# Two layers of state-space model, attention and expert layers on one core: products parted by tile, a second bank for results, constant products ahead of four stages

## The chip, the core and the metric

The kernel runs on one core of one Trainium2 chip, as one launch. The metric is the device time of an execution in microseconds; lower is better. TensorE (PE) multiplies; its weight loads are shown apart (PEld). VectorE (DVE), ScalarE (ACT) and GpSimd (POOL) do the elementwise work, and SyncE (SP) and POOL start transfers.

## The reference

4,096 tokens (8 batches of 512) of width 256 go through two layers. Each layer normalises `xn = layernorm(x)` and adds two branches to `x`:

```python
x = x + mamba(xn)     + one_expert_of_8(xn)             # layer 0
x = x + attention(xn) + two_of_8_experts(xn, capacity)  # layer 1
```

The part that the change touches most is the first branch, for each batch:

```python
z, xBC, dt = xn @ in_proj_w.T
xBC = silu(causal_conv4(xBC)); x, B, C (two directions) = xBC
Y   = ssd(x * dt, A * dt, B, C, chunk=128)        # chunks of 128 tokens, states between them
y   = shift(Y + x * D) forward + backward + x * repeat(x @ fc_D_w.T + D)
out = rmsnorm(y * silu(z)) * norm_w @ out_proj_w.T
```

The attention has 16 heads of width 16: scores of q and k, clipped, multiplied by a decay, clipped, softmax, times v, projected out.

## The kernel before, in words

The kernel is a row of stages, each a block in which every engine has its own instruction stream; a barrier stands between stages. In order: constants, `normalise` and `route` of layer 0 and the time steps (to 93 us of the profiled execution), `mamba` (to 760), `one_expert_each` (to 1084), `normalise` and `route` of layer 1 (to 1173), `project` (to 1276), `attend_and_experts` (to the end). Engines meet only through counting semaphores: `wait_ge` before an instruction, `then_inc` behind it. The order on each engine is the order in which the program is written; there is no planner.

**mamba.** A loop over the 8 batches; a tile is 128 tokens, so a batch has 4 tiles. On PE the function `turn(i, ahead)` makes one batch: the products for `z` (L920, 4 tiles), the turning of B (L931) and of the x rows (L940, one group of four transposes for each tile, copied out by ACT at L1138), the skip factors' products (L947, 8 columns wide, for all tiles into one small part of the bank `psG`), then `products` (C times B, L970), `grow` (the states, L963, three steps in two directions), `diagonal` (L981, then L986 for 8 heads, then L995) for u = 0 to 7 (tile u // 2, direction u % 2), `turn_tile` (L1007) and `output` (L1015) for each tile, and, between these at the end, `conv` (L907), the eight products that the next batch's convolution begins with. ACT makes the decay matrices (`decays`, L1113, 8 exponentials for each u, the first four u without a break). POOL multiplies the x rows by factors: `xdd` (L1204) for the states, `xdt` (L1211) and `xfd` (L1217) for the results. DVE sums neighbours (`near`, L1272), adds D to the skip factors (`fd`, L1275), masks and multiplies the decays (L1299, L1302), carries the states on (L1287 to L1292), and in `finish` reads the finished bank `psY` (L1327), adds and gates; `outputs` (L1342) adds the result to x. `other_taps` (L1255) is DVE's part of the convolution: six additions for each pair of channels' tiles, 128x512.

PSUM has eight banks, all in use: `psA` (two, turned rows and outputs), `psS` (two), `psG`, `psY`, `psO` (two). The convolution's products go round four banks, `psC` = `psS` (two), `psY`, `psA[0]`. Since there is one `psY`, PE's `diagonal` of a tile's first direction waits until DVE has read the tile before:

```python
pe.wait_ge(y_read, i * CPB + t)
```

**one_expert_each.** 39 tiles of rows sorted by expert. POOL issues 12 row fetches and the loads of the second weights before it marks the first expert's weights as there (L1461), and PE's first `down` (L1502) waits for that mark.

**project** makes q, k and v in parts and stores them. **attend_and_experts** goes through 512 tiles of scores in one skewed pipeline: `score` on PE runs 12 tiles ahead, `clip` (L2271) and `fade` (L2279) on DVE follow, `exp` (L2220) on ACT, `turn` (L2111) on PE, its copy (L2229) on ACT, `mix` (L2125); from tile 4 on, one job of the experts (L2163, L2170, L2177) stands behind every fourth tile. There are three score banks, so `score(3)` waits for the first clip. The block `v` (4,096 values a partition) is cleared by POOL's memset (L2072) behind the first loads that POOL issues, and DVE waits for `v_cleared` ahead of its first clip.

## Time and profile before

| | |
|---|---|
| median of 3 runs | 2097.98 us (2097.97 to 2099.04) |
| profiled execution, its own time | 2115.85 us |
| its span, first to last instruction | 2114.1 us |
| mean granted TensorE clock | 0.931 |
| PE busy | 1805.7 us (85%) |
| PEld busy | 1230.2 us (58%) |
| DVE busy | 1376.7 us (65%) |
| ACT busy | 1158.1 us (55%) |
| POOL busy | 419.7 us (20%) |

### The profile page before, as it was taken

The numbers are of one execution on the slowest core, as the hardware profiler recorded it, in microseconds if no ns is written. First come the engines' busy times: TensorE is split into PE (matmuls) and PEld (weight loads), VectorE is DVE, ScalarE is ACT, GpSimd is POOL, SyncE is SP. The second block draws the span as 40 slices with busy tenths as digits, with TensorE's granted clock in tenths as the row PEclk, the third lists the DMA queues.
The fourth block names the chain that finished last, engine by engine and source line by source line (L and its number), as shares of the span: only waits on it lengthen the run. The fifth ranks groups of instructions, "written<-read, shape, count | busy, mean of one in ns | idle before, by whom it ended". The sixth has DMA issues, their size and how long they took to land. (4 is left out here: it accounts for less than half of the span.)

```text
span 2114.1 us, 33649 instructions
## 1 busy us (share of the span) xinstructions
PE 1805.7 (85%) x9950; PEld 1230.2 (58%) x9950; DVE 1376.7 (65%) x3090; ACT 1158.1 (55%) x2806; POOL 419.7 (20%) x406
## 2 busy tenths in 40 slices
PE   5288898898899869899945695998989999999998
PEld 2246666656656669799932353564646565655555
DVE  5647667667667622122246686797878888888885
ACT  2154654664564612122212354888788888788886
POOL 2003313313413432422111202010010202020101
PEclk9589999999999989899977797999999999999999
DMA  4411211211211168455354294233333334333311
GB/s 168 147 59 62 89 63 66 94 65 59 100 68 50 60 223 281 161 175 175 131 160 160 75 296 130 70 82 72 98 72 85 98 84 104 80 91 81 81 31 31
DMA packets 143789, 226.10 MB, mean 107 GB/s; under 512 B 17725, under 2 KB 110015, under 8 KB 143648
## 3 DMA queue, kind: packets, MB, share of 16 engines
q1 hardware_dynamic: 124464, 179.95, 27.4%
q0 software_dynamic: 19184, 44.45, 8.2%
q8 instruction: 67, 1.10, 0.2%
q14 instruction: 74, 0.61, 0.1%
HBM read 174.26 MB, written 50.99 MB: 107 GB/s over the span
## 5 line engine op out<-in xcount | busy, mean ns | idle before, releaser
L2271 DVE TENSOR_SCALAR att_scores<-att_psS 128x512 f32<-128x512 f32 x512 | 349.6, 683 | 106.3 <-PE att_psS L2103 90.9
L2220 ACT ACTIVATE att_prob<-att_scores,att_shift 128x512 f32<-128x512 f32 x512 | 383.2, 748 | 30.7 <-DVE att_shift L2287 30.6
L2229 ACT COPY att_pT<-att_psT 128x512 f32<-128x512 f32 x512 | 305.9, 598 | 136.1 <-PE att_psT L2111 134.9
L2279 DVE CUSTOM_DVE_ANT_0 att_scores<-att_scores,first_decay 128x512 f32<-128x512 f32 x512 | 348.4, 681 | 0.0
L2111 PEld LDWEIGHTS att_psT<-ident,att_prob 128*128 128x128 f32 x2048 | 244.8, 142 | 159.4 <-issue 100.2
L2111 PE MATMUL att_psT<-ident,att_prob 128*128 128x128 f32 x2048 | 315.2, 277 | 15.4 <-ACT att_pT L2229 13.9
L2103 PE MATMUL att_psS<-first_ks,first_qs 128*128 128x512 bf16 x512 | 197.7, 387 | 27.8 <-DVE att_scores L2271 22.6
L1113 ACT ACTIVATE mamba_L<-mamba_am,mamba_minus 128x128 f32<-128x128 f32 x512 | 153.9, 388 | 59.3 <-PE mamba_psY L986 59.2
L2125 PE MATMUL att_psO<-att_pT,att_v 128*32 128x512 f32 x1024 | 139.7, 619 | 37.7 <-ACT att_pT L2229 37.7
L1488 PE MATMUL ffn_psH<-ffn_xT,ffn_w 128*128 128x128 f32 x1248 | 151.0, 280 | 5.0 <-issue 4.4
L1488 PEld LDWEIGHTS ffn_psH<-ffn_xT,ffn_w 128*128 128x128 f32 x1248 | 150.1, 196 | 8.6 <-issue 6.7
L1531 ACT ACTIVATE ffn_hT<-ffn_psH,ffn_b 128x128 f32<-128x128 f32 x156 | 44.6, 368 | 200.7 <-PE ffn_psH L1488 136.3
L1502 PE MATMUL ffn_psY<-ffn_w,ffn_hT 128*128 x624 | 146.0, 386 | 6.0 <-issue 4.9
L1552 DVE TENSOR_SCALAR ffn_hT<-ffn_psH,ffn_b 128x128 f32<-128x128 f32 x156 | 44.1, 345 | 164.0 <-PE ffn_psH L1488 124.6
L1502 PEld LDWEIGHTS ffn_psY<-ffn_w,ffn_hT 128*128 128x128 f32 x624 | 117.1, 193 | 23.4 <-issue 9.3
L986 PE MATMUL mamba_psY<-mamba_xdt,mamba_L 128*128 128x64 f32 x1024 | 121.2, 273 | 0.2 <-POOL mamba_xdt L1211 0.2
L986 PEld LDWEIGHTS mamba_psY<-mamba_xdt,mamba_L 128*128 128x128 f32 x1024 | 120.3, 193 | 0.8 <-issue 0.3
L2170 PE MATMUL att_psF<-att_xT,att_w 128*128 128x512 f32 x224 | 114.1, 634 | 0.0
L1204 POOL TENSOR_TENSOR mamba_xdd<-mamba_xl,mamba_dtdec 128x512 f32<-128x512 f32 x48 | 56.8, 1198 | 273.1 <-ACT mamba_xl L1138 235.2
L2220 ACT ACTIVATION_READ_ACCUMULATOR att_prob<-att_scores,att_shift 128x1 f32 x512 | 110.6, 216 | 0.0
L2177 PE MATMUL att_psF<-att_w,att_hT 128*128 128x256 f32 x448 | 108.5, 385 | 0.0
L2177 PEld LDWEIGHTS att_psF<-att_w,att_hT 128*128 128x128 f32 x448 | 84.5, 192 | 22.4 <-issue 12.2
(283 smaller groups left out, 2820.8 us busy)
## 6 DMA issues: line engine op xcount, KB each, us to landing
ffn_w<-in_w SPq DMA_DIRECT2D x39, 1024.0 KB
mamba_am<-a_rows SPq DMA_DIRECT2D x64, 512.0 KB, 3.8
first_qs<-q_parts SPq DMA_DIRECT2D x256, 64.0 KB
first_ks<-k_parts SPq DMA_DIRECT2D x256, 64.0 KB
xn<-xn_all SPq DMA_DIRECT2D x16, 512.0 KB, 5.8
ffn_w<-in_w POOLq DMA_DIRECT2D x8, 1024.0 KB, 6.1
att_w<-in_inter POOLq DMA_DIRECT2D x7, 1024.0 KB, 5.6
att_w<-in_outer POOLq DMA_DIRECT2D x7, 1024.0 KB
```

Source lines behind the costliest of these rows:

```text
L986: mm = nc.tensor.matmul(psY[:, h * HD:(h + 1) * HD], L[:, u % NL, h], xdt[:, u % 2, h * HD:(h + 1) * HD], start=False, stop=(d == 1), skip ...
L1113: ex = nc.scalar.activation(L[:, u % NL, h], am[:, u % NA, h * P:(h + 1) * P], ACT.Exp, bias=minus[:, d, t, h:h + 1])
L1488: mm = nc.tensor.matmul(psH[j % 2][hf][:, q], w1[:, j % NW, k, (hf * HALF + q) * P:(hf * HALF + q + 1) * P], xT[:, j % 2, k], start=(k == ...
L1502: mm = nc.tensor.matmul(psY[j % 2][:], hT[:, j % 2, f], w2[:, bass.ds(at * W2N + f * D, D)], start=(f == 0), stop=(f == FT - 1))
L2103: nc.tensor.matmul(psS[n % NS][:], qs[:, of % NQK, j, t * P:(t + 1) * P], ks[:, of % NQK, j, :], start=True, stop=True).then_inc(scored, 1)
L2111: mm = nc.tensor.transpose(ps[:, k * P:(k + 1) * P], prob[:, n % NP, k * P:(k + 1) * P], C.ident[:])
L2125: mm = nc.tensor.matmul(psO[STRIP * j:STRIP * (j + 1), :], v[:, b % 2, k, octet * QUAD + j, i], pT[:, (of * QUAD + j) % HEADS_T, k], start ...
L2177: mm = nc.tensor.matmul(psF[:, 0:D], hT[:, f, t * P:(t + 1) * P], w2[:, f], start=(f == 0), stop=(f == FT - 1), skip_group_check=True)
L2220: nc.scalar.activation(prob[:, n % NP], scores[:, n % NCL], ACT.Exp, bias=shift[:, h % 2, t:t + 1], accum_out=total[:, octet % 2, t, j, i: ...
L2229: nc.scalar.copy(pT[:, h % HEADS_T, :, t * P:(t + 1) * P], bank_of("turn", n)[:].rearrange("p (k q) -> p k q", k=CPB)).then_inc(pT_ready, 1)
L2271: vec.tensor_scalar(scores[:, n % NCL], psS[n % NS][:], -CLAMP, CLAMP, ALU.max, ALU.min).then_inc(clipped, 1)
L2279: vec.tensor_tensor_reduce(scores[:, n % NCL], scores[:, n % NCL], decay[:, FAR - t * P:FAR - t * P + SEQ], 1.0, -2.0 * CLAMP, ALU.mult, A ...
```

## The change

Five edits:

1. **Skip factors by tile.** `skips(t)` makes the eight instructions of one tile. Two tiles' stand between the turnings of the x rows, two behind the first two steps of `grow`. The rows are turned in the order 0, 3, 1, 2 (`TURN`); POOL begins each of its first four `xdd` when that tile's rows are there, not when all are. DVE's `fd` stands behind `grow(1)`.
2. **Two result banks.** `psG` is given up; its table moves to `psO[1]`, its skip factors to `psY[1]`. A tile's results go to `psY[t % 2]`.
3. **The convolution's fourth bank** is `psY[1]`, no longer `psA[0]`, so waits around `psA` change; the last `turn_tile` no longer waits for four results of the next batch's convolution.
4. **Constant products.** `keep_running` multiplies a block of ones by the identity into a bank whose content isn't needed: 16 times at the beginning of `mamba` and `one_expert_each`, 14 times in `project`, and 14 times in attention behind the third score. Nothing reads them.
5. **Attention's values cleared first.** POOL's memset stands ahead of its loads, and DVE waits for it in `spread_values(0)` (tile 6), no longer ahead of the first clip.

```diff
+def keep_running(nc, C, bank, times):
+    for _ in range(times):
+        nc.tensor.matmul(bank, C.ones[:], C.ident[:], start=True, stop=True)
...
+    TURN = [0, 3, 1, 2]
...
-        psG = s.psum("psG", [P, 512])
-        psY = s.psum("psY", [P, DI])
+        psY = [s.psum(f"psY{j}", [P, DI]) for j in range(2)]
...
-        psC = [ps[:].rearrange("p a b -> p (a b)") for ps in psS] + [psY[:], psA[0][:]]
+        psC = [ps[:].rearrange("p a b -> p (a b)") for ps in psS] + [ps[:] for ps in psY]
-        fd_ps = psG[:, 448:480].rearrange("p (c h) -> p c h", c=CPB)
+        fd_ps = psY[1][:, 0:CPB * NH].rearrange("p (c h) -> p c h", c=CPB)
-        psP = psG[:, 0:L0_TILES]
+        psP = psO[1][:, 0:L0_TILES]
...
+                keep_running(nc, C, psO[0][:, 0:P], 16)
...
-                    elif n == 2:
-                        pe.wait_ge(y_read, i * CPB)
-                    elif n == 3:
+                    elif n < 4:
                         if not_first:
-                            pe.wait_ge(yT_ready, i * CPB - 1)
+                            pe.wait_ge(y_read, i * CPB + n - 3)
...
-                    for t in range(CPB):
-                        use = XT_AT + t
+                    def turn_rows(k):
+                        use, t = XT_AT + k, TURN[k]
...
+                    pe.wait_ge(fd_ready, i)
+                    turn_rows(0)
+                    turn_rows(1)
+                    skips(0)
+                    turn_rows(2)
+                    skips(1)
+                    turn_rows(3)
...
-                            pe.wait_ge(y_read, i * CPB + t)
+                            if t >= 2:
+                                pe.wait_ge(y_read, i * CPB + t - 1)
+                            elif t == 1:
+                                pe.wait_ge(fd_ready, i + 1)
...
                     products(0)
                     grow(0)
+                    skips(2)
                     products(1)
                     grow(1)
+                    skips(3)
                     grow(2)
...
-                    turn_tile(CPB - 1, ahead)
+                    turn_tile(CPB - 1)
...
-                    pool.wait_ge(tok_ready, (i + 1) * (2 + CPB))
                     for k in range(CPB - 1):
                         for d in range(2):
                             n = 2 * k + d
+                            if n < CPB:
+                                pool.wait_ge(tok_ready, i * (2 + CPB) + 2 + n + 1)
...
-                    dve.wait_ge(fd_done, i + 1)
-                    dve.wait_ge(xfd_ready, i * CPB)
-                    v.tensor_tensor(fd[:], fd_ps, ...).then_inc(fd_ready, 1)
                     grow(1)
+                    dve.wait_ge(fd_done, (i + 1) * CPB)
+                    dve.wait_ge(xfd_ready, i * CPB)
+                    v.tensor_tensor(fd[:], fd_ps, ...).then_inc(fd_ready, 1)
                     grow(2)
...
+                keep_running(nc, C, psY[0][:, 0:P], 16)        # one_expert_each
...
+                keep_running(nc, C, psV[0][:, 0, 0:P], 14)     # project
...
+                nc.gpsimd.memset(v[:], 0.0).then_inc(v_cleared, 1)
                 load_rows(0)
                 load_w1(0)
                 load_w2(0)
-                nc.gpsimd.memset(v[:], 0.0).then_inc(v_cleared, 1)
...
+                        if n + SCORE == NS - 1:
+                            keep_running(nc, C, psF[:, 0:P], 14)
...
+                    if b == 0:
+                        dve.wait_ge(v_cleared, 1)
...
-                dve.wait_ge(v_cleared, 1)
```

## Rows read from the trace of the kernel before

**Rows 1.** The page: TensorE's granted clock in forty slices, in tenths
```profile
PEclk9589999999999989899977797999999999999999
```

**Rows 2.** PE's waits, 143 to 755 us: total us, times, longest
```profile
PE mamba_psY L981 <- DVE mamba_y L1327: 26.2, 24, 1.4
...
PE mamba_psO L963 <- POOL mamba_xdd L1204: 14.0, 8, 2.3
...
PE mamba_psA L1007 <- DVE mamba_acc L1255: 9.9, 7, 1.4
```

**Rows 3.** Timeline, PE, one batch: start, length, line, count, [idle before <-releaser]
```profile
384.25 3.80 PE L947 MATMUL mamba_psG<-mamba_w_fcd,mamba_xc 128*128 128x8 f32 x32
...
388.90 2.92 PE L963 MATMUL mamba_psO<-mamba_xdd,mamba_Bl 128*128 128x512 f32 x4
...
407.32 1.16 PE L981 MATMUL mamba_psY<-mamba_d_diag,mamba_near 128*128 128x128 f32 x8 [1.38 <-DVE mamba_y L1327]
...
433.14 3.60 PE L907 MATMUL mamba_psS<-mamba_xT,mamba_w_in 128*128 128x512 f32 x8
...
446.75 0.66 PE L1007 MATMUL mamba_psA<-ident,mamba_y 128*128 128x128 f32 x4 [1.41 <-DVE mamba_acc L1255]
```

**Rows 4.** Timeline, DVE, the same batch
```profile
389.70 1.23 DVE L1302 SCALAR_TENSOR_TENSOR mamba_L<-mamba_L,mamba_masked 128x1024 f32<-128x1024 f32 x1
...
408.63 1.22 DVE L1302 SCALAR_TENSOR_TENSOR mamba_L<-mamba_L,mamba_masked 128x1024 f32<-128x1024 f32 x1
```

**Rows 5.** Timeline, ACT, the same batch
```profile
385.06 1.28 ACT L1113 ACT_TABLE_LOAD   x1
...
386.35 9.46 ACT L1113 ACTIVATE mamba_L<-mamba_am,mamba_minus 128x128 f32<-128x128 f32 x32
```

**Rows 6.** Stretches: us; busy (count) of PE, PEld, DVE, ACT, POOL; granted clock
```profile
388.00:391.00 3.00, 3.00 (x8) 1.91 (x8) 1.92 (x4) 3.00 (x11) 0.10 (x1) 0.50 0.38 116
...
397.00:401.00 4.00, 3.65 (x10) 2.11 (x9) 3.67 (x6) 0.00 (x0) 3.73 (x3) 0.60 0.31 124
...
1288.00:1297.00 9.00, 4.84 (x8) 0.83 (x8) 9.00 (x23) 2.31 (x7) 0.00 (x0) 0.50 0.24 85
```

**Rows 7.** Timeline, beginning of the state-space stage
```profile
99.53 7.05 PE L387 MATMUL mamba_psG<-mamba_table_valued,mamba_table_hot_row 128*128 128x39 f32 x32 [7.39 <-POOL mamba_table_valued L366]
...
106.38 6.02 PE L907 MATMUL mamba_psS<-mamba_xT,mamba_w_in 128*128 128x512 f32 x8
...
113.24 4.28 DVE L1255 SCALAR_TENSOR_TENSOR mamba_acc<-mamba_psS,mamba_taps,mamba_acc 128x511 f32<-128x511 f32 x6 [10.01 <-ACT mamba_acc L1081]
...
115.66 1.87 PE L387 MATMUL mamba_psG<-mamba_table_valued,mamba_table_hot_row 128*128 128x39 f32 x16
```

**Rows 8.** Timeline, beginning of the one-expert stage
```profile
780.21 0.15 POOL L1461 MEMSET ffn_marked<- 128x1 f32 x1
...
780.50 3.72 PE L1502 MATMUL ffn_psY<-ffn_w,ffn_hT 128*128 x16 [1.05 <-POOL ffn_marked L1461]
```

**Rows 9.** ACT's waits, 755 to 1075 us: total us, times, longest
```profile
ACT ffn_hT L1531 <- PE ffn_psH L1488: 136.3, 29, 5.0
...
ACT ffn_hT L1531 <- DMA xnT<-norm_xT: 20.3, 1, 20.3
```

**Rows 10.** Timeline, PE, beginning of the projections
```profile
1178.44 1.97 PE L1729 MATMUL proj_psV<-proj_wd,proj_wkT 128*128 128x64 f32 x8 [16.03 <-DVE proj_wkT L1823]
...
1180.79 3.68 PE L1700 MATMUL proj_psL<-xT_all,proj_wkv 128*64 128x512 f32 x4 [0.38 <-DVE proj_wkv L1825]
...
1184.40 4.63 PE L1707 MATMUL proj_psQ<-xT_all,proj_wq 128*128 128x512 f32 x8
```

**Rows 11.** Timeline, beginning of attention
```profile
1276.61 1.44 PE L2103 MATMUL att_psS<-first_ks,first_qs 128*128 128x512 bf16 x3 [4.26 <-PEq L66]
...
1284.22 3.53 POOL L2072 MEMSET att_v<- 128x4096 f32 x1
...
1287.85 1.89 DVE L2271 TENSOR_SCALAR att_scores<-att_psS 128x512 f32<-128x512 f32 x3 [14.87 <-POOL att_v L2072]
```

More of the change, by code:

```diff
@@ L820, in drained @@
             if last < BT_AT:
-                eng.wait_ge(conv_done, (i + 1) * CT)
+                eng.wait_ge(yT_ready if last % 2 == 0 else o_ready, i * CPB)
             elif last < TAIL_AT:
@@ L942, in turn, with skips @@
                         mm.then_inc(bank_ready, 1)
-                    pe.wait_ge(fd_ready, i)
-                    for t in range(CPB):
+                    def skips(t):
                         for m in range(DI // P):
@@ L948, in turn @@
                                                   start=(m == 0), stop=(m == DI // P - 1))
-                    mm.then_inc(fd_done, 1)
+                        mm.then_inc(fd_done, 1)
+                    pe.wait_ge(xc_ready, (i + 1) * CT)
+                    pe.wait_ge(fd_ready, i)
[5 more added lines that the diff above has]
+                    turn_rows(3)
                     def grow(k):
@@ L976, in diagonal @@
                         if d == 0:
-                            pe.wait_ge(y_read, i * CPB + t)
+                            if t >= 2:
+                                pe.wait_ge(y_read, i * CPB + t - 1)
+                            elif t == 1:
+                                pe.wait_ge(fd_ready, i + 1)
                             pe.wait_ge(near_ready, i + 1)
                             for m in range(DI // P):
-                                nc.tensor.matmul(psY[:, m * P:(m + 1) * P], near[:, m, t * P:(t + 1) * P], d_diag[:, m],
+                                nc.tensor.matmul(psY[t % 2][:, m * P:(m + 1) * P], near[:, m, t * P:(t + 1) * P], d_diag[:, m],
                                                  start=(m == 0), stop=False, skip_group_check=True)
@@ L985, in diagonal @@
                         for h in range(NH):
-                            mm = nc.tensor.matmul(psY[:, h * HD:(h + 1) * HD], L[:, u % NL, h], xdt[:, u % 2, h * HD:(h + 1) * HD],
+                            mm = nc.tensor.matmul(psY[t % 2][:, h * HD:(h + 1) * HD], L[:, u % NL, h], xdt[:, u % 2, h * HD:(h + 1) * HD],
                                                   start=False, stop=(d == 1), skip_group_check=True)
@@ L996, in diagonal, with turn_tile @@
                                              start=True, stop=True).then_inc(off_ready, 1)
-                    def turn_tile(t, after_conv=False):
+                    def turn_tile(t):
                         use = TAIL_AT + 2 * t
-                        if after_conv:
-                            pe.wait_ge(conv_done, (i + 1) * CT + 4)
-                        else:
-                            drained(pe, i, use)
+                        drained(pe, i, use)
                         pe.wait_ge(gated, i * CPB + t + 1)
@@ L1048, in _ @@
                 for n in range(CT):
-                    conv(0, n, n != 3)
+                    conv(0, n, False)
                     if n in (3, 5):
@@ L1132, in batch @@
                         nc.scalar.copy(Bl[:, d], psA[(BT_AT + d) % 2][:].rearrange("p (t n) -> p t n", t=CPB)).then_inc(tok_ready, 1)
-                    for t in range(CPB):
-                        act.wait_ge(bank_ready, i * USES + XT_AT + t + 1)
+                    for k in range(CPB):
+                        act.wait_ge(bank_ready, i * USES + XT_AT + k + 1)
                         act.wait_ge(xdt_ready, i * U)
                         act.wait_ge(xfd_ready, i * CPB)
-                        nc.scalar.copy(xl[:, t], psA[(XT_AT + t) % 2][:]).then_inc(tok_ready, 1)
+                        nc.scalar.copy(xl[:, TURN[k]], psA[(XT_AT + k) % 2][:]).then_inc(tok_ready, 1)
                     act.wait_ge(minus_ready, i + 1)
```

9 lines of the change are left out of this document (2 added, 7 removed).

## The prediction

> **What bounds the kernel now.** The page comes first. PE is busy 85% of the span, more than any other engine, and its granted clock stands in nearly every slice at 9 [rows 1], so short stretches at the low level, 0.50 or 1.2 GHz, are spread over the whole kernel. The question is where PE waits, and where it works at half speed.
>
> PE's waits in the state-space stage [rows 2] hold three large entries: 26.2 us in 24 equal waits (three a batch) for DVE's read of the result bank, 14.0 us for POOL's xdd, 9.9 us in seven waits ahead of the last turned tile. Then the timeline of one batch. PE makes the skip factors without a break, 3.80 us, and the first states begin at 388.90 and run slowly [rows 3]; the wait for the result bank at 407.32 and the one at 446.75 follow [rows 3]. The stretches give the clock: the low level from 388 to 391, right behind the narrow skip products, and again for most of 397 to 401, behind PE's wait for xdd [rows 6]. Last, the beginnings of the four stages [rows 7, 8, 10, 11]. In attention DVE's first clip starts at 1287.85, released by the memset, though the first three scores ran from 1276.61 [rows 11].
>
> **The second result bank.** With it `diagonal` of tiles 1 to 3 no longer waits for the read just ahead of it. The three waits of a batch go: 26.2 us in all [rows 2]. What is late next? DVE. In the batch shown L(3) is ready at 408.63 + 1.22 = 409.85 [rows 4]. PE needs it one `products` after the end of the second direction's work; its sequence, 1.38 us earlier than before from 407.32 on, reaches that point at 410.0, so there is room for 0.15 us only. Later tiles have more: PE needs about 9 us a tile with no waits, DVE some 7.6 us. I take 26.0 us. If DVE's order does bind, each of the three waits comes back in part; lower bound 8 us, upper 29.
>
> **The convolution's fourth bank.** The last turned tile no longer waits 1.41 us for four results [rows 3]. But conv 6 behind it waits for the third of them, one addition of 0.7 us earlier than the fourth, and the last `output` needs a copy that stands on ACT behind the silu of that pair. PE does the transposes in the old wait, then waits some 0.25 and 0.15 us. Gain 1.0 us in each of seven batches, 7 us (bounds 3 and 9.9, the entry of [rows 2]). The last batch has no convolution ahead.
>
> **Skips parted, rows turned in another order, xdd earlier.** No work is removed: 32 instructions at 3.80 / 32 = 0.12 us each [rows 3] stay. Two tiles' skips, 1.9 us, now stand between the turnings, partly in waits of 0.6 us, so the last x rows reach ACT about 1.55 us later. ACT's table load, which follows at 385.06, and its exponentials move by as much [rows 5]: eight exponentials take 9.46 / 4 = 2.37 us, so the first L can be multiplied at 385.06 + 1.55 + 1.28 + 2.37 = 390.3, where it was 389.70 [rows 4]. DVE keeps its order, so the states behind it begin 0.6 us later. They get part of it back, since the first states' products are early and xdd no longer late: DVE's idle moment between the first two copies goes, and L(1) starts perhaps 0.2 us later than before. `fd`, formerly ahead of everything in idle time, adds 0.25 us to the chain. POOL's earlier xdd avoids some of the sharing that slowed DVE's L(1). The chain of states thus ends within 0.3 us of where it ended: the 14.0 us of waits for xdd are exchanged for waits for DVE's states, and I book nothing for them.
>
> What remains is PE's own work around the chain. If its clock is back at the full level when the last step of `grow` runs, the last products end 0.9 us earlier and the four neighbour products another 0.6. If the level is low while skips(3) runs, these eight take about 1.8 us, stand ahead of the last `grow`, and hold `fd` and the last two states up: a loss of 1.3 us. I take a gain of 0.3 us a batch, 2 us in all; ends, 8 x -1.3 = -10 and 8 x 1.7 = +14.
>
> **Constant products, state-space stage.** The table's 32 instructions wait for POOL until 99.53, then take 7.05 us at the low level, 0.22 us each; at the full level 16 take 1.87, so 0.12 each. The first two convolution products take 6.02 [rows 7] where they take 3.60 at the full level [rows 3]. DVE's additions wait for them until 113.24 and then run for the rest of the stage's beginning, so their start sets it. The constant products begin at about 94, fill the wait and don't delay the table. If the level stays full, the gain is 7.05 - 3.74 + 6.02 - 3.60 = 5.7 us. But they are through at about 98 if they run at the full level, and then comes a gap and narrow work, as the skips are: the low level can be back before the convolution. Bounds 0 and 5.7; I take 4.0, nearer to the upper since only one of several parts would be lost.
>
> **One expert.** PE's 16 constant products, at most 7 us, lie in its wait for the first rows. What they gain in the first `up` is hidden: the first `down` waits 1.05 us for the mark, which POOL sets at 780.21 behind its own queue of issues [rows 8]. Booked at 0. Without that cover it would be 2.6 us; the longer wait ahead of 780.5 could let the clock fall, at a cost up to 2.
>
> **Projections.** PE is idle 16.03 us ahead of 1178.44 and then works at the low level: 1.97, 3.68, 4.63 us [rows 10]. At the full level the same shapes take 8 x 0.12 = 0.9, 1.9 and 3.7 (512 columns at 3.60 / 8 = 0.45 each [rows 3]). The stage begins at about 1173.6; 28 constant instructions take 28 x 0.22 = 6.2 us low, 3.3 full; at 5.5 they end 0.7 us behind the old start. What is saved is 3.7 less 0.7; a small wait for DVE between the first two takes another 0.3: 2.7 us (bounds 0.5 and 3.7). PE paces that stage, and its stores shift with it.
>
> **Attention.** DVE's clip no longer waits for the memset: score 0 is there at about 1277.1, 10.7 us ahead of 1287.85 [rows 11]. Not all of it is kept. PE issues the constant products behind the third score, from 1278.05 on, 28 instructions, 5.5 us, and score(3) is behind them. Clip(3) stood three clips (1.89 us) and a fade behind the first, at 1290.3; now it can start at 1278.05 + 5.5 + 0.4 = 1283.95. Gain 6.4 us (5.6 if all 28 run low, 8.4 if all run full). The memset, 3.53 us [rows 11], now delays POOL's first row fetches and weight loads against the stage's start; their users are the experts' jobs from tile 4 on, over 12 us later, so that costs nothing; without the cover it would be 3.5 us less 6.4. The whole in-order pipeline behind shifts.
>
> For the clock, between 1288 and 1297 PE was busy 4.84 of 9.00 us with single scores and stayed at 0.50 [rows 6]; after the constant products the same sparse scores follow, so I book no gain for it. The Trainium skill, "TensorE: Matmul & The Clock Gate", section "HAM oscillation — how this bites in real kernels", says that a matmul engine left waiting goes back to its half clock and pays anew in each burst; by that rule, with which the 0.50 of these 9 us agrees, the constant products of attention buy nothing that lasts and only stand in front of score 3. The sum stays as it is, and the fourth rival below becomes less likely.
>
> **The sum.** 26 + 7 + 2 + 4 + 0 + 2.7 + 6.4 = 48.1 us. The profiled execution's own time is 2115.85, 1.75 over its span and 17.87 over the median. ACT's one wait of 20.3 us, where its like last at most 5.0 [rows 9], is a stall of all engines near 852 to 872 that adds some 15 us; I take it that the timed runs lack it. A profiled execution with the same stall would take 2115.85 - 48.1 = 2067.8; against the median, 2097.98 - 48.1 = 2049.9 us.
>
> **The rivals.**
> - *As forecast*: 2050, by its own range 2042 to 2059. Chance 0.47.
> - *The skips meet the low clock.* PE idles more between the states than before, so skips(3) runs low in each batch: -10 in place of +2, and perhaps the stage's beginning at 0. For it: the low level behind the skips at 388 [rows 6]. Against: its part is only a quarter as long. Time 2062 to 2066. Chance 0.22.
> - *DVE becomes the bound.* The margin of 0.15 us at L(3) is lost and the waits for y turn into waits for L. Only 8 of 26 us stay: 2068. Against it: DVE is busy less than PE. Chance 0.13.
> - *The clock no longer falls.* The low stretches of a batch, 3 us from 388 and over 3 us of 397 to 401 [rows 6], vanish; half of these 6.2 us is work at half speed, of which at most 1.7 us a batch lie on the path: 14 in place of 2, and 5.7 in place of 4: 2036. Chance 0.12.
> - *Slower.* PE's level stays low past the states, into the `diagonal` work that follows. One us at the low level there costs 0.5 us. To eat 48 us and 4 more it must last 13 us longer in each batch than now; from there on the kernel is slower, at 20 us by 8 x 10 - 48 = 32 us: 2130. Against: the work behind 401 is dense. Chance 0.03.
> - *Nothing changes*: the states' chain gives back what the bank gains. 2098. Chance 0.03.
>
> A measurement of this kernel can tell about 0.2%, or 4 us. Faster by more than that has 0.94, within it 0.03, slower 0.03. The range 2035 to 2068 leaves out 0.06 of these cases on the slow side and the tails of the others.
>
> **What would show it.** In the trace after, PE's L981 should hardly wait for DVE's L1327; if a wait for L1302 stands there, DVE binds. L1007's wait for L1255 should be gone and L907 show short ones. L963's waits should name L1290 or L1292, not L1204. The clock from 390 to 401 of a batch decides between the second and fourth case. DVE's first L1255 should start 4 us nearer to the stage's start; the clips at attention's start 0.7 us behind the stage's start, with a gap of about 4 us before the fourth. The mark at L1461 should stand as far behind its stage's start as now, with PE waiting longer for it. The prediction is wrong if the batch's period falls by less than 3 us or by more than 6.

## The result and the profile after

The changed kernel takes 2044.46 us (median of 4 runs, 2040.12 to 2049.56), the kernel before 2098.23 us beside it (2097.97 to 2099.04). The ratio is 0.9744, with a 95% interval from 0.9715 to 0.9773: 54 us less. The four runs stand in two pairs, 2040.1 and 2040.8 against 2048.1 and 2049.6, with mean granted clocks of 0.944 and 0.945 against 0.942 and 0.940. The profiled execution is one of the upper pair, 2049.56 us with a span of 2047.8; no execution of the lower pair was profiled, so what parts the two is read below from other profiles (at "The clearing behind the loads again"). Of all executions in this document one, of the kernel with the last turned tile late, ran at a mean granted clock of 0.749 (2368.9 us) and is left out of that kernel's median.

The page of the changed kernel: busy time of PE, and the granted clock in forty slices, to be laid beside [rows 1].

```profile
PE 1803.0 (88%) x10070; PEld 1240.1 (61%) x10070; DVE 1381.2 (67%) x3090; ACT 1159.0 (57%) x2806; POOL 432.4 (21%) x406
...
PEclk9689899899899889999966999999999999999999
```

PE's share has risen from 85 to 88%, since waits went. The dips of the state-space stage are still there.

The length of each stage, from its first DMA issue to that of the next, in the two profiled executions:

| stage | before | after | change | forecast |
|---|---|---|---|---|
| ahead of the state-space stage | 93.8 | 94.2 | +0.4 | 0 |
| state-space | 666.5 | 626.0 | -40.5 | -39 |
| one expert | 323.7 | 309.0 | -14.7 | 0, and -15 for the stall |
| norm and routing | 89.6 | 89.8 | +0.2 | 0 |
| projections | 103.0 | 100.0 | -3.0 | -2.7 |
| attention | 837.5 | 828.8 | -8.7 | -6.4 |

Inside the state-space stage the first z product stands 39.3 us behind the stage's start (39.9 before), the eight batches repeat every 76.2, 74.9, 72.0, 74.8, 72.0, 74.8 and 72.0 us (before 82.9, then 77.7 to 78.8), and 70.0 us follow the last z product (73.2). So the 40.5 us are 0.6 + 36.7 + 3.2.

PE's waits in that stage of the changed kernel, 130 to 735 us (total us, times, longest), against [rows 2]:

```profile
PE mamba_psO L972 <- DVE mamba_state L1300: 23.1, 8, 3.0
...
PE mamba_psY L910 <- DVE mamba_acc L1266: 1.7, 7, 0.2
```

The 26.2 us of waits for the result bank have left no entry at all. The 9.9 us ahead of the last turned tile have become 1.7 us ahead of the convolution. The 14.0 us for POOL's xdd have become 23.1 us for DVE's first states, 2.9 in each batch. What follows this longer wait is seen in two kinds of batch that stand side by side. PE's timeline of the changed kernel, first a batch with period 72.0, then one with 74.8:

```profile
303.10 3.37 PE L972 MATMUL mamba_psO<-mamba_xdd,mamba_Bl 128*128 128x512 f32 x4 [2.88 <-DVE mamba_state L1300]
306.30 0.95 PE L947 MATMUL mamba_psY<-mamba_w_fcd,mamba_xc 128*128 128x8 f32 x8
307.11 1.96 PE L972 MATMUL mamba_psO<-mamba_xdd,mamba_Bl 128*128 128x512 f32 x4
308.91 1.05 PE L993 MATMUL mamba_psY<-mamba_d_diag,mamba_near 128*128 128x128 f32 x8
...
375.05 3.75 PE L972 MATMUL mamba_psO<-mamba_xdd,mamba_Bl 128*128 128x512 f32 x4 [2.88 <-DVE mamba_state L1300]
378.59 1.71 PE L947 MATMUL mamba_psY<-mamba_w_fcd,mamba_xc 128*128 128x8 f32 x8
380.16 3.76 PE L972 MATMUL mamba_psO<-mamba_xdd,mamba_Bl 128*128 128x512 f32 x4
383.71 1.41 PE L993 MATMUL mamba_psY<-mamba_d_diag,mamba_near 128*128 128x128 f32 x8
```

And the stretches of both (us; busy time and count of PE, PEld, DVE, ACT, POOL; granted clock; DMA):

```profile
304.00:306.00 2.00, 2.00 (x4) 0.89 (x3) 1.88 (x3) 2.00 (x9) 0.78 (x1) 0.51 0.71 238
306.00:308.00 2.00, 2.00 (x11) 1.33 (x11) 1.88 (x5) 2.00 (x8) 1.72 (x3) 1.00 0.50 195
...
376.00:378.00 2.00, 2.00 (x4) 0.93 (x3) 1.88 (x4) 2.00 (x8) 0.82 (x1) 0.50 0.68 248
378.00:380.00 2.00, 2.00 (x9) 1.48 (x8) 1.45 (x3) 2.00 (x8) 1.33 (x3) 0.50 0.66 205
...
382.00:384.00 2.00, 2.00 (x5) 0.96 (x4) 1.67 (x2) 0.00 (x0) 1.37 (x2) 0.50 0.39 162
```

Both batches wait 2.88 us; in both the clock falls before the wait is over (the granted clock is 1.00 from 300 to 302 and 0.63 from 302 to 304, and 1.00 from 372 to 374 and 0.55 from 374 to 376), and both do grow(1) at the low level. In the first the full level is back at 306, and skips(3), grow(2) and the near products take 0.95, 1.96 and 1.05 us; in the second it comes back at 384, and they take 1.71, 3.76 and 1.41. That is 2.9 us more, about the difference of the two periods (2.8). In this execution five of the eight batches have the long form. The two batches have the same instructions and the same waits up to this point; what decides between the forms no run shows.

The beginnings of the other stages of the changed kernel. State-space, against [rows 7]:

```profile
94.28 3.81 PE L110 MATMUL mamba_psO<-ident,ones 128*128 128x128 f32 x32 [1.75 <-PEq L66]
99.92 5.96 PE L394 MATMUL mamba_psO<-mamba_table_valued,mamba_table_hot_row 128*128 128x39 f32 x32 [1.83 <-POOL mamba_table_valued L373]
105.67 6.51 PE L910 MATMUL mamba_psS<-mamba_xT,mamba_w_in 128*128 128x512 f32 x8
...
113.03 3.63 DVE L1266 SCALAR_TENSOR_TENSOR mamba_acc<-mamba_psS,mamba_taps,mamba_acc 128x511 f32<-128x511 f32 x5 [9.41 <-ACT mamba_acc L1091]
```

One expert, against [rows 8]:

```profile
720.28 6.43 PE L110 MATMUL ffn_psY<-ident,ones 128*128 128x128 f32 x32 [4.51 <-PEq L66]
...
728.14 3.81 PE L1499 MATMUL ffn_psH<-ffn_xT,ffn_w 128*128 128x128 f32 x32 [0.55 <-ACT ffn_xT L1534]
...
740.10 0.13 POOL L1472 MEMSET ffn_marked<- 128x1 f32 x1
740.38 6.61 PE L1513 MATMUL ffn_psY<-ffn_w,ffn_hT 128*128 x16 [3.00 <-POOL ffn_marked L1472]
```

Projections, against [rows 10]:

```profile
1119.10 6.24 PE L110 MATMUL proj_psV<-ident,ones 128*128 128x128 f32 x28 [11.27 <-PEq L66]
1125.17 1.00 PE L1742 MATMUL proj_psV<-proj_wd,proj_wkT 128*128 128x64 f32 x8
1126.56 1.93 PE L1712 MATMUL proj_psL<-xT_all,proj_wkv 128*64 128x512 f32 x4 [0.38 <-DVE proj_wkv L1838]
1128.42 3.70 PE L1719 MATMUL proj_psQ<-xT_all,proj_wq 128*128 128x512 f32 x8
```

Attention, against [rows 11]:

```profile
1219.05 3.51 POOL L2082 MEMSET att_v<- 128x4096 f32 x1 [64.21 <-POOLq L66]
...
1219.08 1.44 PE L2116 MATMUL att_psS<-first_ks,first_qs 128*128 128x512 bf16 x3 [3.63 <-PEq L66]
1220.32 5.11 PE L110 MATMUL att_psF<-ident,ones 128*128 128x128 f32 x28
...
1231.34 0.61 PE L2116 MATMUL att_psS<-first_ks,first_qs 128*128 128x512 bf16 x1 [0.89 <-DVE att_scores L2286]
...
1219.78 1.89 DVE L2286 TENSOR_SCALAR att_scores<-att_psS 128x512 f32<-128x512 f32 x3 [3.70 <-PE att_psS L2116]
...
1225.68 0.69 DVE L2286 TENSOR_SCALAR att_scores<-att_psS 128x512 f32<-128x512 f32 x1 [3.40 <-PE att_psS L2116]
```

The projections and attention go as written down ahead, attention by 2.3 us better. The state-space beginning does not: the table's and the convolution's products are for the most part at the low level in spite of the constant ones (5.96 and 6.51 us; 7.05 and 6.02 before). In the one-expert stage the first down product takes 6.61 us where it took 3.72.

### The profile page after: what moved, and what is told of

Its sections match the earlier page's. It is cut to its first block and busy times, and to the rows that moved or that the text cites. A ratio compares the mean times of both kernels' runs of the same rounds, so it can differ in the third digit from the quotient of the medians.

```text
span 2047.8 us, 33896 instructions
## 1 busy us (share of the span) xinstructions
PE 1803.0 (88%) x10070; PEld 1240.1 (61%) x10070; DVE 1381.2 (67%) x3090; ACT 1159.0 (57%) x2806; POOL 432.4 (21%) x406
## 5 line engine op out<-in xcount | busy, mean ns | idle before, releaser
L1499 PEld LDWEIGHTS ffn_psH<-ffn_xT,ffn_w 128*128 128x128 f32 x1248 | 145.3, 192 | 3.6 <-DMA ffn_w<-in_w 0.9
L1499 PE MATMUL ffn_psH<-ffn_xT,ffn_w 128*128 128x128 f32 x1248 | 145.8, 275 | 1.2 <-DMA ffn_w<-in_w 0.7
L1310 DVE SCALAR_TENSOR_TENSOR mamba_L<-mamba_L,mamba_masked 128x1024 f32<-128x1024 f32 x64 | 92.1, 1440 | 30.8 <-ACT mamba_L L1123 28.1
L1215 POOL TENSOR_TENSOR mamba_xdd<-mamba_xl,mamba_dtdec 128x512 f32<-128x512 f32 x48 | 50.2, 1060 | 269.7 <-ACT mamba_xl L1148 212.7
```

Of the source, the lines that this page charges most:

```text
L1499: mm = nc.tensor.matmul(psH[j % 2][hf][:, q], w1[:, j % NW, k, (hf * HALF + q) * P:(hf * HALF + q + 1) * P], xT[:, j % 2, k], start=(k == ...
```

## Experiments

Twelve kernels, in three groups, each on one chip with the kernel before beside them. In group one (the first four kernels) the kernel before takes 2114.52 us (median of 7), and the one-expert stage lasts 321 to 327 us in the profiles of all four, so ratios to the kernel before and stages are compared rather than totals. The changed kernel itself was not run in this group; its ratio is the 0.9744 of the first comparison, its stages those of its profile above. In groups two and three (the rest) the kernel before takes 2095.4 us and the one-expert stage is free of that stall (306 to 309 us). Stage lengths and periods are of the profiled executions, one for each kernel, while the medians are of all its runs.

**One result bank again.** Each tile's products wait for the read just ahead, in the changed kernel:

```diff
-                            if t >= 2:
-                                pe.wait_ge(y_read, i * CPB + t - 1)
-                            elif t == 1:
-                                pe.wait_ge(fd_ready, i + 1)
+                            pe.wait_ge(y_read, i * CPB + t)
+                            if t == 1:
+                                pe.wait_ge(fd_ready, i + 1)
```

> The kernel after, but PE's diagonal of a tile waits again until DVE has read the tile just before, as with one result bank (both banks stay). Theory, the wait itself is the price: three waits a batch come back, 1.38 + 0.94 + 0.94 us, so 8 x 3.26 = 26 us slower than the kernel after, near 2070, and each batch's period 3.3 us longer, with PE's L993 waiting for DVE's L1335. Rival, DVE paces the tiles anyway: less than 8 us slower.

2092.25 us, ratio 0.9885 [0.9844, 0.9927]; state-space stage 663.7 us, periods 78.4 to 78.5 us from the second on. PE's waits in that stage, and its timeline of one batch:

```profile
PE mamba_psY L992 <- DVE mamba_y L1334: 26.1, 24, 1.4
```

```profile
388.48 3.75 PE L972 MATMUL mamba_psO<-mamba_xdd,mamba_Bl 128*128 128x512 f32 x4 [2.88 <-DVE mamba_state L1299]
392.02 1.72 PE L947 MATMUL mamba_psY<-mamba_w_fcd,mamba_xc 128*128 128x8 f32 x8
393.59 3.76 PE L972 MATMUL mamba_psO<-mamba_xdd,mamba_Bl 128*128 128x512 f32 x4
```

The waits are back to a tenth of a microsecond, 26.1 for 26.2. But in this profile the stage is 37.7 us longer, not 26. All eight batches now have skips(3) at 1.7 us, the long form, three more than before; at 2.9 us each that is 8.7 of the 11.6 us beyond the waits, and the other 2.9 are not traced. The profiled execution is also the slowest of the four (2107.51 us; the others 2084.15, 2084.75 and 2099.74). By the ratios, 0.9885 for 0.9744, the waits cost 1.4% or about 30 us over all runs, give or take some 10, which the theory's 26 fits.

**The last turned tile late again.** In the changed kernel, one line ahead of the last `turn_tile`:

```diff
+                    if ahead:
+                        pe.wait_ge(conv_done, (i + 1) * CT + 4)
                     turn_tile(CPB - 1)
```

> The kernel after, but the last turned tile of a batch waits again for four results of the next batch's convolution. Theory: a seventh of 7 us each, so 7 us slower than the kernel after (1.0 us a batch in seven batches), since in the kernel after PE waits some 0.4 us behind that place instead. Rival: the whole 1.41 us comes back, 9.9 us. Second rival: 0, since DVE's additions pace the convolution.

2071.63 us (median of three), ratio 0.98 [0.9769, 0.9831]; stage 635.1 us, 9.1 longer, with the old wait of 9.9 us in seven parts. That lies between the theory's 7 and the first rival's 9.9, and nearer to the rival; six of the eight batches have the long form, one more than in the changed kernel.

**No constant products at all**, the four calls of `keep_running` taken out:

```diff
-                keep_running(nc, C, psO[0][:, 0:P], 16)
...
-                keep_running(nc, C, psY[0][:, 0:P], 16)
...
-                keep_running(nc, C, psV[0][:, 0, 0:P], 14)
...
-                        if n + SCORE == NS - 1:
-                            keep_running(nc, C, psF[:, 0:P], 14)
```

> The kernel after without any of the constant products. The four stages are parted by barriers, so each stage's length tells its own. Theory: the state-space stage 0.7 us longer, the one-expert stage 2.9 us shorter (its first second-layer products, 6.61 us at the low clock in the kernel after, go back to 3.7), the projections 2.8 us longer, attention 4.5 us shorter (score 3 no longer stands behind 28 instructions). In all 3 to 4 us faster than the kernel after. Rival, the constant products help wherever PE is about to begin: each stage 2 to 4 us longer, in all 10 us slower.

2064.0 us, ratio 0.9746 [0.9712, 0.978]. The first z product stands 39.4 us behind the stage's start (39.3 with them), the projections last 103.7 us (100.0), attention 824.0 us (828.8). Attention's first exponential stands 7.6 us behind the stage's start, with the constant products 11.1. So these pay in the projections and cost in attention. The state-space stage is 628.3 us long (626.0), the one-expert stage 327.3, which the stall keeps from being read. Over the whole kernel the ratio is that of the changed kernel, 0.9744; with intervals of 0.003 to either side that speaks against the rival's 10 us and doesn't show the theory's 3 to 4.

**The skips together again**, behind the turned rows, with `fd` ahead of the states; the banks stay:

```diff
-                    turn_rows(0)
-                    turn_rows(1)
-                    skips(0)
-                    turn_rows(2)
-                    skips(1)
-                    turn_rows(3)
+                    for k in range(CPB):
+                        turn_rows(k)
+                    for t in range(CPB):
+                        skips(t)
...
                     grow(0)
-                    skips(2)
                     products(1)
                     grow(1)
-                    skips(3)
                     grow(2)
```

> The kernel after, but the skip factors' products stand together behind the turned rows and DVE's addition of D ahead of the states, as before; the rows' order 0, 3, 1, 2, POOL's early start and the two banks stay. Theory: PE's clock falls behind the narrow products as before, at the first states; the chain of states starts as early as ACT's exponentials allow, 1.5 us earlier than in the kernel after. Period between 72 and 75 us, within 8 us of the kernel after either way. Rival, the parting is what makes the change fast: 3 us a batch, 24 us slower.

2049.86 us, ratio 0.9702 [0.9679, 0.9724]; periods 74.9, 74.3, 72.3, 74.3, 72.1, 72.5, 74.3; stage 620.9 us, of which 3.3 less than before lie ahead of the first z product (36.0 us behind the start). PE waits 16.2 us for POOL's xdd and 4.7 for DVE. The periods are between 72 and 75 us and the ratio is 0.4% below that of the changed kernel, as the theory has it, not 24 us slower. Parting the skips, as it was done, brings nothing that this shows; the periods alternate either way.

**The changed kernel again**, unchanged, as the base of group two.

> The changed kernel unchanged, as the base for the others on one chip. Both theories expect the ratio of the first comparison again, 0.974 within 0.003, a state-space stage of about 626 to 628 us, batch periods that alternate between about 74.8 and 72.0 us, and 829 us of attention.

2037.54 us (2035.17 to 2048.28, 5 runs), ratio 0.9735 [0.9714, 0.9757]; periods 73.8, 72.0, 72.0, 72.0, 74.9, 72.0, 74.9, and a stage of 617.6 us. The ratio is as expected, the stage is 8 us shorter than expected: the same instructions met another clock. PE's timeline at the stage's beginning:

```profile
97.69 4.22 PE L394 MATMUL mamba_psO<-mamba_table_valued,mamba_table_hot_row 128*128 128x39 f32 x32 [1.83 <-POOL mamba_table_valued L373]
101.71 4.93 PE L910 MATMUL mamba_psS<-mamba_xT,mamba_w_in 128*128 128x512 f32 x8
```

Behind the same constant products and the same gap of 1.83 us the table takes 4.22 us, not 5.96, and the first z product stands 36.0 us behind the start. The runs again split, four near 2037 (mean granted clock 0.946 to 0.948) and one at 2048 (0.941). Of the 12.0 us between this profiled execution and that of the first comparison, 3.3 lie ahead of the first z product and 5.3 in the periods.

**Skips(3) early**, in PE's wait for the first states:

```diff
                     products(1)
+                    skips(3)
                     grow(1)
-                    skips(3)
                     grow(2)
```

> Skips(3) stands ahead of grow(1), in the wait of 2.9 us for the first states, and not behind it. Theory A (what is left of the skips' cost is that skips(3) stands ahead of the last grow while the clock is at the low level): the last grow starts 1 to 1.7 us earlier in the batches with the low clock, periods of 74.8 fall to 72 to 73.5, the stage gets 3 to 8 us shorter than in the changed kernel. Rival B (DVE's chain of states sets the last grow, and PE's skips only fill its waits): the periods stay within 0.3 us and the stage within 2 us, whatever stands where. Rival C (dense work in the wait keeps the clock up): every period goes to 72.0 and the stage to about 618.

2032.21 us (2030.29 to 2033.98), ratio 0.9701 [0.9688, 0.9715]; stage 611.1 us, periods 73.8, 71.9, 72.0, 72.0, 72.4, 72.1, 73.7. PE's timeline of one batch and a stretch of it:

```profile
362.61 0.96 PE L947 MATMUL mamba_psY<-mamba_w_fcd,mamba_xc 128*128 128x8 f32 x8
365.65 4.35 PE L972 MATMUL mamba_psO<-mamba_xdd,mamba_Bl 128*128 128x512 f32 x6 [2.09 <-DVE mamba_state L1300]
```

```profile
366.00:368.00 2.00, 2.00 (x3) 0.80 (x3) 1.88 (x4) 2.00 (x8) 0.22 (x1) 0.50 0.57 201
368.00:370.00 2.00, 2.00 (x4) 0.30 (x2) 1.88 (x3) 2.00 (x9) 1.61 (x2) 0.82 0.58 193
```

Skips(3) takes 0.96 us in all eight batches. The wait is 2.1 us instead of 2.9; the clock still falls in it, but in the batch shown comes back within grow(1). Some batches now wait for POOL's xdd instead, 3.2 us in five waits. The stage is 6.5 us shorter than in the run beside it, the runs lie within 3.7 us instead of 13. Theory A, close to rival C.

**The clearing behind the loads again**; the wait for it stays at the first use of the values:

```diff
-                nc.gpsimd.memset(v[:], 0.0).then_inc(v_cleared, 1)
                 load_rows(0)
                 load_w1(0)
                 load_w2(0)
+                nc.gpsimd.memset(v[:], 0.0).then_inc(v_cleared, 1)
```

> The clearing of attention's values stands behind the loads again, while DVE still waits for it only at the first use of the values and not ahead of the first clip. Theory A (attention's beginning gained from the place of the wait alone): first clips and first exponential as in the changed kernel within 0.5 us, attention within 2 us of 829. Rival B (the place of the clearing matters too: POOL's first loads are 3.5 us late in the changed kernel and hold the first experts): attention is 2 to 4 us shorter than in the changed kernel. Rival C (the clearing then comes late for the first use): attention 2 us longer.

2045.89 us, ratio 0.9756 [0.9732, 0.9779]; attention 827.3 us (827.1 in the run beside it), first exponential at 11.2 (11.0) us. Theory A: what paid in attention is that DVE's first clip no longer waits; where POOL clears is worth nothing. The median is 8 us above that of the run beside it all the same, and this pair of profiles tells what parts the two groups of times. The runs split again (2039.29 and 2041.47, 2050.31 and 2051.45), the profiled one is of the upper pair (2050.31), the one beside it of the lower (2037.54), and both ran the same instructions in the state-space stage. It lasts 628.5 us for 617.6: 10.9 of the 12.8 us between the two executions, 3.3 ahead of the first z product and 7.6 in the periods, with six batches of the long form for three.

**Skips together, constant products ahead of the projections alone**: the fourth kernel's edit, and three of the four calls of `keep_running` taken out.

> The skips stand together behind the turned rows, as before the change, and of the constant products only those ahead of the projections are left. Theory A (parts add up: constant products cost about 5 us ahead of attention, 3 us ahead of the first down product of the one-expert stage, bring nothing in the state-space stage and 3.7 us in the projections; together skips bring 4 to 9 us): about 5 us below the run with the skips together alone (2049.9), so 2042 to 2047, ratio 0.966 to 0.968, attention 819 to 824 us. Rival B (the gain of the run with the skips together came from the full clock at the stage's beginning, which the constant products helped): first z product 39.4 us behind the stage's start instead of 36.0, ratio about 0.969 to 0.971.

2038.21 us, ratio 0.9731 [0.9717, 0.9745]; one-expert stage 306.2 us (309.0 with its constant products), attention 823.7 (827.1), first z product 39.3 us behind the start. The two stages are 2.8 and 3.4 us shorter, as theory A says, but the ratio is above what either expected and is that of the changed kernel, which has the skips parted and all the constant products: the skips together bring none of the 4 to 9 us taken from the fourth kernel, whose stage's beginning had met the full level. The 39.3 us are rival B's. One-expert stage of this kernel:

```profile
733.69 0.15 POOL L1467 MEMSET ffn_marked<- 128x1 f32 x1
...
721.75 5.88 PE L1494 MATMUL ffn_psH<-ffn_xT,ffn_w 128*128 128x128 f32 x32 [0.55 <-ACT ffn_xT L1528]
...
733.98 3.71 PE L1508 MATMUL ffn_psY<-ffn_w,ffn_hT 128*128 x16 [1.55 <-POOL ffn_marked L1467]
```

Without the constant products the first up takes 5.88 us instead of 3.81, and nobody waits for it; the wait for the mark is 1.55 us instead of 3.00, and the first down takes 3.71 instead of 6.61.

**Skips early, constant products only in the state-space stage and the projections**: the sixth kernel without two of its calls.

> Skips(3) ahead of grow(1), and no constant products in the one-expert stage and in attention; those of the state-space stage and of the projections stay. Theory A (the parts add up): one-expert stage 306 instead of 309 us, attention about 823.5 instead of 826.5, so 6 us below the run with the early skips, ratio 0.967 to 0.968. Rival B (each removed part is taken back by the clock behind it): ratio 0.970 again.

2028.45 us (2027.22 to 2036.9), ratio 0.968 [0.9663, 0.9697]; one-expert stage 306.1 us. Attention's first exponential is at 7.6 us, but the profiled execution lost the 3.5 us again between there and the last one (802.7 us, 799.4 in the run of the changed kernel). The ratio is the one of theory A, though its interval reaches to rival B's. The median is 9.1 us below that of the changed kernel, and the two intervals stand apart: the fastest version, with the next.

**More constant products ahead of the table**, 26 for 16, in that kernel:

```diff
-                keep_running(nc, C, psO[0][:, 0:P], 16)
+                keep_running(nc, C, psO[0][:, 0:P], 26)
```

> The same kernel with 26 instead of 16 constant instructions at the start of the state-space stage, which fill PE's last wait of 1.8 us before the table's products. Theory A (whether the first convolution products meet the low clock hangs on the gap of 1.8 us and falls either way from one execution to the next): without the gap the first z product stands 36 us behind the stage's start in each execution, and the runs spread less. Rival B (the narrow table products let the clock fall, whatever stands ahead of them): 39.3 us still occurs, the ratio is that of the kernel with 16 within 0.1%.

2029.61 us, ratio 0.9687 [0.9669, 0.9704]. PE's timeline at the stage's beginning:

```profile
93.81 6.04 PE L110 MATMUL mamba_psO<-ident,ones 128*128 128x128 f32 x52 [1.75 <-PEq L66]
99.69 3.66 PE L394 MATMUL mamba_psO<-mamba_table_valued,mamba_table_hot_row 128*128 128x39 f32 x32
103.18 5.38 PE L910 MATMUL mamba_psS<-mamba_xT,mamba_w_in 128*128 128x512 f32 x8
```

The gap is gone and the table is at the full level, yet the convolution behind it still falls to the low one. The first z product stands at 36.2 us. The runs spread over 6.5 us, those of the kernel with 16 over 9.7 (four of the five within 1.6), so no smaller spread is shown, and the median is the same. One profile doesn't decide between the theories for the gap. That the clock fell behind narrow work without any gap is seen in it: PE is busy for all of 99 to 107 us, with a granted clock of 1.00 to 103 and 0.57 from there on.

**One bank with the skips together**: the fourth kernel's edit and the first one's.

> The skips together behind the turned rows as before the change, and each tile's diagonal products wait for the read just ahead again, as with one result bank. Theory A (the bank is worth its own waits, and the 37 us of the first such run came from the parted skips, which then met the low clock in every batch): 26 to 29 us more in the state-space stage than with the skips together and two banks, so about 648 us of stage, periods about 3.3 us longer. Rival B (with the waits PE's clock falls in any order of the skips): 36 to 40 us more, 658 us.

2075.25 us, ratio 0.9896 [0.9874, 0.9918]; stage 652.3 us, seven periods that sum to 542.0 against 514.6 with two banks: 27.4 us, and 31.4 for the stage, 3.3 of which are the beginning's other clock. Against the eighth kernel, with the same 39.3 us at the beginning, the stage is 30.9 us longer (621.4). Theory A: the waits for the read are 26.2 us in all eight batches, and what comes on top is 2 to 5 us and not 12.

**Early skips, constant products ahead of the projections alone**: the ninth kernel ("the first kernel" of the text below) without those of the state-space stage.

> As the first kernel of this call, without the constant products of the state-space stage too. Theory A (they bring 3.3 us in some executions and nothing in the others): the first z product 39.3 us behind the stage's start in the profile, ratio 0.0005 to 0.001 above the first kernel's. Rival B (they bring nothing, the first convolution's clock falls either way without them): 36.0 may occur here too, ratio the same.

2032.22 us, ratio 0.9699 [0.9677, 0.9721]; first z product 39.3 us behind the start. Against the same kernel with the 16 constant products of the state-space stage (0.968): theory A's direction, 0.002, within the two intervals. Against the eighth kernel, which differs from it in the skips' place alone (together, 0.9731), the early skips bring 0.3%, 6 us in the medians, though the ends of the two intervals overlap; the stage lasts 614.4 us for 621.4, with the first z product at 39.3 in both.

## Why the prediction was right

Forecast 2050 us in 2035 to 2068, measured 2044.46. By its own steps:

- **The second result bank, 26 us.** Right. Its 26.2 us of waits [rows 2] went and came back with one bank as 26.1; with the skips together the bank is worth 27 to 31. The 24 waits are not equal, as the text has them, but 1.38, 0.94 and 0.94 us in each batch; their sum is the same. The margin of 0.15 us ahead of DVE's L(3) held: no wait for L or y stands among PE's waits. What the term missed is that more waiting can go with more batches of the long form: undone in the changed kernel, the bank costs 37.7 us in the profile, where all eight batches have that form instead of five, and about 30 over all runs.
- **The convolution's fourth bank, 7 us.** Right in kind, a little small. 9.9 us of waits became 1.7, 8.2 saved; undone it costs 9.1. The estimate of 0.25 and 0.15 us of new waits was 0.24 in all.
- **Skips parted, 2 us between -10 and +14.** Both cases of the text occur, batch by batch. Taking off the 3.3 and 1.2 us a batch of the two terms above, a batch of 74.8 us lost 0.9 against 78.4 (the text: 1.3), one of 72.0 won 1.9 (the text: 1.7). The three terms together, 39.9 us in the profiled execution, were forecast as 35, so about 5.5 are left for this one. They don't come from the parting: with the skips together the periods are the same 72 to 75 us. Whether they come from the rows' order, POOL's earlier xdd or the clock, no run parts. That the 14.0 us for xdd are exchanged for waits for DVE was also right; their growth to 23.1 was not foreseen, and it is in this wait that the clock falls. Two rivals, "the skips meet the low clock" and "the clock no longer falls", therefore don't exclude each other: their batches alternate in one execution, and how many of each it gets makes much of the difference between its faster and its slower executions. That the batches mix and so come out near the middle of the range is luck: the text has one case or the other in every batch.
- **State-space constant products, 4.0 us.** The step that failed in the profiled execution: 0.6 us, and 0.1 against the same kernel without constant products (39.3 and 39.4 us). With the 16 constant products the first z product is some 3.3 us earlier in three of nine profiles, without them in none of four (and with 26 in the one there is), so an estimate of the term over executions is 3.3 x 3 / 9, about 1 us. The warning that narrow work behind a gap may bring the low level back before the convolution was the right one; the value taken, near the upper bound, was too hopeful.
- **One expert, 0.** Mis-sized: it costs 2.9 us. The gain in the first up was hidden as said. The longer wait did let the clock fall (0.50 from 740 to 746), "at a cost up to 2"; the first down products took 6.61 us for 3.71. A cost named but not booked.
- **Projections, 2.7 us.** Measured 3.0 between the two profiles and 3.7 with the products taken out. The constant products took 6.24 us where the text has 5.5, so the first of the stage's own begin 6.1 us behind its start and not 4.8; the rest of the stage made up for it.
- **Attention, 6.4 us.** Measured 8.7. The clips stand 0.7 us behind the stage's start with a gap of 3.4 us before the fourth, as written; the fourth clip and the first exponential are 7.0 us nearer to the start. That no lasting clock is won is right too: at 1231.34 a score takes 0.61 us again, behind waits of 0.4 to 0.9 us, with a granted clock of 0.50 from 1231 to 1237 where it was 0.99 from 1224 to 1231. The Trainium skill, "TensorE: Matmul & The Clock Gate", section "HAM oscillation — how this bites in real kernels", says that a waiting matmul engine pays for its clock anew in each burst; its case has one long wait a round, this one many short ones, and this row agrees. The constant products cost 3.5 us at the stage's beginning (11.1 against 7.6). The clearing's new place is worth nothing; what pays is the new place of the wait for it. The other 1.7 us no experiment parts: the time from the first to the last exponential went from 802.9 to 799.8, and it scatters by more from one kernel to the next (795 to 806).
- **The profiled execution's 15 us.** Right, and a little small. The stage that held the stall is 14.7 us shorter in the profile, 2.9 of constant products included, so the stall was about 17.6 us; 323.7 against the 306.1 us of the kernels that have neither gives the same, and the profiled execution stood 17.87 us over the median. It was not a stall of all engines: between 852 and 869 ACT stands, as does DVE to 872 but for one instruction; PE goes on slowly, a few products at a time with pauses that nothing in the profile releases, and POOL issues its transfers as before.

Its own sign, that the batch's period falls by 3 to 6 us, holds for the mean (73.8 for 79.1) and not for each batch: from 78.4 the long ones fell by 3.6, the short ones by 6.4.

The errors partly cancel, and that is luck: 3.4 and 2.9 us too hopeful in two stages' beginnings, about 5 and 2.3 us too careful in the batches and in attention. The sum of the terms as measured, 40.5 - 2.9 (in the one-expert stage, whose stall hides it in the profiles) + 3.0 + 8.7 = 49.3 us, against 48.1 forecast, fits this execution's 2049.6; the faster pair of runs gained some 9 us more.

## What to carry to other kernels

A wait that a second buffer removes can be priced from its own row. Here the wait itself came back to 0.1 us when it was undone, and the time by 27 to 38 us for 26: what can't be read off the row is whether the pauses that remain leave the matmul engine's clock at its low level for the work behind, so look at what stands right behind the longest remaining pause. Fill that pause with work that is ready anyway (skips(3) moved into it: 5 and 6 us in two comparisons), rather than put the same work behind it. In this kernel constant products paid only in the projections, where the stage's own dense work follows them directly and is on the path; ahead of a second wait, in the one-expert stage, they made that wait longer and cost more than they won. And where two executions of one kernel differ by 0.5%, a stage's length in one profile is no better than that either.

## What the runs showed of the hardware

- Behind the same wait of 2.88 us the same instructions met the low level for longer in some batches (skips(3) at 1.71 us) than in others (0.95), in a pattern that changes from one execution to the next: five long batches of eight in one profile of the changed kernel, three in the other. Batch periods were 74.8 and 72.0 us, and the times of the one kernel stand in two groups 0.5% apart, the slower group with the lower mean clock. In the two profiles of group two that differ in nothing but attention's clearing, 2050.31 and 2037.54 us, the state-space stage with six and three long batches makes 10.9 of the 12.8 us. What starts the one pattern or the other is open.
- Narrow products at full occupancy (39 columns, 32 in a row, no gap) were followed by the low level in the convolution: 5.38 us where 3.60 is the full level's. In the kernel before the low level also comes right behind 32 narrow products in a row, 3.80 us of 8 columns each [rows 3, rows 6].
- The stall in the one-expert stage of the profile before [rows 9] does not hang on the kernel: every profile of group one has it (321 to 327 us of stage), no profile of groups two and three (306 to 309). In the first comparison the profiled execution of the kernel before has it (323.7), the profile of the changed kernel has not (309.0), and the timed runs of the kernel before stand 17 to 18 us below its profiled execution. What causes it is open; no part of the change brings or removes it.
